# The same units on five engines, taken in another order: a kernel of four streams

## Chip, cores and metric

The kernel runs on one core of a Trainium2 chip. The time is the device time of one execution in microseconds; the kernel before took 561.78, 567.68 and 565.25 us in three runs, median 565.25.

## What is computed

128 sequences of 32 tokens with 128 features go through four layers; a conditioning vector of 128 features comes with each sequence. Cut to what matters:

```python
# layer 0: graph attention, twice (adjacency and its transpose), over the first 20 tokens
self_feat = concat(x, q if x.sum(-1) != 0 else 0) @ W_self.T + b_self
aff = where(adj.sum(-1) > 0, q_h @ k_h / sqrt(8), NEG) + adj @ w_bias + b_bias   # 16 heads
x = x + relu(self_feat + sum over d of (softmax(aff) @ self_feat[:20]) @ Wout[d])
# layer 1: x += gate * causal attention(modulated norm(x)); x += gate * (gelu(xm @ W1) @ W2)
# layer 2: x += gate * (gelu(xm @ w1) @ w2);  x += gate * (gelu_tanh(xm @ w1) @ w2)
# layer 3: as layer 1 without the causal mask
```

## The kernel before

The 128 sequences are eight chunks of 16, and a chunk is 512 token rows, held as tiles of 128 x 512 f32. Chunk c belongs to stream c % 4, so there are four streams, each with its own buffers and its own two banks of PSUM, and each does two chunks one after the other. A fifth lane holds the setup.

A chunk is a fixed list of stages (`chunk_stages`): the row sum and self product, keys and values, scores, softmax, turn (the transpose of the probabilities on DVE), values products, divide, and, for each of six blocks (attention, MLP with 4, 1 and 2 hidden products, attention, MLP with 4), stats, norm, modulate, then the attention's stages with gather and project, or the hidden products and down, and residual at the end. Each engine executes its own part of a stage; that part is a unit here. "Bias" is an addition on POOL (L678) of a gated bias that SP loads with the gate (`q_gate<-gates_out`, L570) before the block's residual (L682). `vals` on SP (L580) are four copies of the values into a block-diagonal tile, without which PE's values products can't start. `next_adj` (L529) loads the next chunk's 704 KB of adjacency.

What an engine does in which order is written out: `MERGE` has a string of digits for each engine, and each digit says from which lane (0 to 3 a stream, 4 the setup) the next unit is taken. Within a lane the order is that of the stages. `order` turns a string into a list of units, and at its end each engine's program is a loop over its list:

```python
def order(engine, merge):
    turns = [iter(lane) for lane in lanes(engine)]
    assert [merge.count(str(n)) for n in range(NS + 1)] == [len(lane) for lane in lanes(engine)]
    return [next(turns[int(s)]) for s in merge]
...
            for kind, a, c in ORDERS["gpsimd"]:
                stage(kind, a, c)
```

A unit begins with its waits for semaphores, which count what other engines and transfers have done for this stream, and a unit at the head of an engine's queue holds up all behind it. A PSUM bank is reused when its reader on ACT or DVE has counted: of four hidden products the fourth needs that the GELU (L798) of the second has run. ACT executes exponentials (L784), the GELUs of both kinds, tanh in the setup, and plain copies with scale and bias. The loops over these lists stand at L594 (SP), L692 (POOL), L801 (ACT), L974 (DVE) and L1183 (PE).

Of the kernel before, what the change touches and what calls it, by code (L numbers as in the profile page):

```python
# [160 lines left out]
def order(engine, merge):  # L161
# [2 lines left out]
    return [next(turns[int(s)]) for s in merge]  # L164

MERGE = {
    "tensor": ("001020420142012402044200420402042230011321302020103303221113013010120323112032000020123213212130"
               "310012112123220300103113210131203023032130112003222010313112330223120121100312302302213013033020"
               "110220223232303012320011233232310111021032122132312332310330223313131131213133023311322303201202"
               "122301132103232121312012330130311111323330331200101203013231121232331030101321331320312001012133"  # L170
               "0230312021120112301303032030223220200000"),
    "vector": ("000142201204041202400204200032030012012132203210320321021013120110310321122120323303210231110213"
               "310310100320233121330123021300213021200120100132321232123130123202312231003100212311333320323021"
               "310233020202212323110210202331312311130133133131232213232023201021113013313103102332031210313121"
               "2301320311322013330120131013310302130122312320230020102000320"),
    "scalar": ("444040044214240020404414224220404130120033210311033231012020000212312130101212320100332121011323"
               "002130102322101213303232111023200301123323001022322001330023232131112230212110333322131331132333"
               "101233212020231102133102223132103111132033331001203012311232103320131331103200321032120012131010"
               "323033220220000"),
    "gpsimd": ("120201020232104044203012010323123321102002010132103102020302131031001300122021201231231231220133"  # L180
               "212010021012013133031323023223230231003112321012312323301302312231310231233013212331013012321322"
               "31011231103232033110023113212123310123031213232013031303200021030101231033212020030320120"),
    "sync": ("020044402231101302230111202313000213232120010321022331123120331203331132202113031032131230130132"
               "21002031320"),
}
ORDERS = {engine: order(engine, merge) for engine, merge in MERGE.items()}

# [1057 lines left out]
```

## Time and profile before

| | |
|---|---|
| median of three runs | 565.25 us (561.78 to 567.68) |
| the profiled execution | 570.62 us, span 568.7 us |
| PE, DVE, ACT, POOL busy | 84%, 76%, 67%, 69% of the span |
| granted clock of TensorE, mean | 0.954 of full speed |
| DMA | 53.43 MB, q1 busy 31.5% of 16 engines |

A row of the timeline begins with the start and the duration in us, then engine, line, operation, tiles written and read, and count; what stands in brackets is the idle time of the engine before it and who ended it. PE is the matmuls, PEld their weight loads, DVE VectorE, ACT ScalarE, POOL GpSimd, SP SyncE, which only issues transfers.

### The profile page before, as it was taken

Reading aid. Unit: us, or ns where it says so; the run is one execution under the profiler, and the core shown is the slowest. Engines: PE = TensorE matmul, PEld = TensorE weight load, DVE = VectorE, ACT = ScalarE, POOL = GpSimd, SP = SyncE. Lnnn points to the kernel's source line nnn. Section 1 sums busy time; section 2 is a strip of 40 time slices with the busy share of each in tenths; the row PEclk is TensorE's granted clock in tenths of the full one; section 3 lists DMA queues with packets and bytes.
Section 4 is the critical chain, followed back from the end, with each engine's and each line's share of the span. In section 5 each row is a group of like instructions: output and inputs, shape, how many; then the busy total and the mean of one; then the engine's idle time right before and its main releaser. Section 6 shows DMA issues by size and latency. Waiting matters only on the chain.

```text
span 568.7 us, 21089 instructions
## 1 busy us (share of the span) xinstructions
PE 476.4 (84%) x9062; PEld 324.6 (57%) x9062; DVE 429.7 (76%) x914; ACT 383.0 (67%) x633; POOL 392.8 (69%) x408
## 2 busy tenths in 40 slices
PE   5877686898899789888899988767899988887996
PEld 2445354566557566465566555455576665565674
DVE  5888899899728856966899967898995454688841
ACT  7895375657587848666796836745866656686961
POOL 2768666667567879559887848655649899755546
PEclk9989898999599969999999987998999999899999
DMA  8514134123042620451433330212344232153321
GB/s 290 194 42 159 60 85 117 47 77 97 9 106 76 199 82 1 117 147 56 128 100 108 111 86 23 68 39 61 112 122 111 75 82 69 28 139 89 94 78 75
DMA packets 23468, 53.43 MB, mean 94 GB/s; under 512 B 5840, under 2 KB 8144, under 8 KB 23376
## 3 DMA queue, kind: packets, MB, share of 16 engines
q1 hardware_dynamic: 22912, 51.14, 31.5%
q8 instruction: 72, 1.18, 0.9%
q10 hardware_dynamic: 432, 0.94, 0.4%
q0 software_dynamic: 32, 0.01, 0.1%
q14 instruction: 20, 0.16, 0.1%
HBM read 39.74 MB, written 2.88 MB: 75 GB/s over the span
## 4 chain that ended last, share of the span: by engine, by line
POOL 27%; DVE 24%; PE 24%; issue 11%; ACT 6%; DMA 4%; SPq 4%; POOLq 0%; DVEq 0%; ACTq 0%
POOL x L682 5%; PE work L1169 5%; POOL x L678 4%; POOL rstd L672 4%; PE work L1178 4%; POOL xm L689 4%; DVE prob L932 4%; PE work L1128 4%; DVE mx L925 3%; POOL kbd L656 3%; POOL prob L667 2%; SPq L580 2%; PE work L1101 2%; DVE prob L927 2%; PE work L1048 2%
## 5 line engine op out<-in xcount | busy, mean ns | idle before, releaser
L793 ACT ACTIVATE xn<-x,nmr,rstd 128x128 f32<-128x128 f32 x192 | 78.5, 482 | 41.4 <-POOL nmr L675 41.3
L1169 PE MATMUL work<-xm,w_layer 128*128 128x512 f32 x176 | 91.5, 634 | 10.4 <-POOL xm L689 9.7
L1178 PEld LDWEIGHTS work<-w_layer,prob 128*128 128x128 f32 x704 | 83.0, 195 | 12.8 <-ACT prob L798 8.7
L1178 PE MATMUL work<-w_layer,prob 128*128 128x128 f32 x704 | 86.8, 280 | 2.3 <-ACT prob L798 2.2
L798 ACT ACTIVATE prob<-work,first 128x512 f32<-128x512 f32 x88 | 58.7, 684 | 42.7 <-PE work L1169 42.5
L678 POOL TENSOR_TENSOR x<-x,q_gate 128x512 f32<-128x512 f32 x48 | 60.8, 1273 | 31.7 <-DMA q_gate<-gates_out 31.7
L932 DVE STREAM_TRANSPOSE prob<-prob 128x1024 f32<-128x1024 f32 x64 | 78.4, 1232 | 2.5 <-ACT prob L784 2.5
L682 POOL TENSOR_TENSOR x<-x,q_gate 128x512 f32<-128x512 f32 x48 | 60.7, 1271 | 24.1 <-DVE q_gate L971 24.0
L689 POOL TENSOR_TENSOR xm<-turned_in,mod 128x512 f32<-128x512 f32 x48 | 50.6, 1056 | 30.1 <-DVE turned_in L966 30.1
L1128 PE MATMUL work<-vbd,prob 128*32 128x36 f32 x4096 | 52.6, 208 | 21.8 <-issue 10.2
L1128 PEld LDWEIGHTS work<-vbd,prob 128*32 128x32 f32 x4096 | 46.1, 117 | 41.1 <-issue 27.2
L784 ACT ACTIVATE prob<-prob 128x1024 f32<-128x1024 f32 (+1 forms) x64 | 56.2, 894 | 16.5 <-POOL prob L667 13.5
L956 DVE BATCH_NORM_STATS2 stats<-x 128x6 f32<-128x128 f32 x192 | 41.4, 278 | 27.2 <-POOL x L682 27.1
L971 DVE TENSOR_TENSOR q_gate<-work,q_gate 128x512 f32<-128x512 f32 x48 | 32.5, 681 | 35.3 <-PE work L1178 28.4
L667 POOL TENSOR_TENSOR prob<-prob,mx 128x640 f32<-128x640 f32 x32 | 40.7, 1271 | 24.3 <-DVE mx L922 24.2
L966 DVE TENSOR_TENSOR turned_in<-work,mod 128x512 f32<-128x512 f32 x48 | 32.5, 680 | 25.3 <-PE work L1144 25.3
L672 POOL TENSOR_TENSOR rstd<-veps,neg_half 128x4 f32<-128x4 f32 x48 | 48.8, 1017 | 3.7
L1169 PEld LDWEIGHTS work<-xm,w_layer 128*128 128x128 f32 x176 | 29.7, 196 | 37.0 <-POOL xm L689 15.3
L1144 PE MATMUL work<-ident,xn 128*128 128x128 f32 x192 | 41.3, 303 | 9.7 <-ACT xn L793 7.2
L1144 PEld LDWEIGHTS work<-ident,xn 128*128 128x128 f32 x192 | 25.4, 146 | 31.4 <-ACT xn L793 28.3
L925 DVE TENSOR_REDUCE mx<-work 128x32 f32<-128x1024 f32 x32 | 38.8, 1213 | 5.5 <-PE work L1101 5.5
L656 POOL TENSOR_TENSOR kbd<-turned_in,graph_mask 128x1280 f32<-128x1280 f32 x16 | 37.5, 2347 | 5.9 <-ACT turned_in L760 4.0
(138 smaller groups left out, 933.9 us busy)
## 6 DMA issues: line engine op xcount, KB each, us to landing
q_gate<-gates_out SPq DMA_DIRECT2D x192, 128.0 KB, 2.9
vbd<-v_ev SPq DMA_DIRECT2D x128, 72.0 KB, 2.4
kbd<-in_adj SPq DMA_DIRECT2D x8, 704.0 KB, 5.0
turned_in<-in_x_tok SPq DMA_DIRECT2D x8, 256.0 KB, 3.0
out_x<-x SPq DMA_DIRECT2D x8, 256.0 KB, 2.2
turned_in<-in_x_feat SPq DMA_DIRECT2D x7, 256.0 KB, 4.5
w_layer<-in_weights SPq DMA_DIRECT2D x2, 768.0 KB, 5.3
w_layer<-in_modw SPq DMA_DIRECT2D x1, 768.0 KB, 7.4
```

Of the source, the lines that this page charges most:

```text
L672: pool.tensor_tensor(rstd[s][:], veps[s][:], neg_half[:], ALU.pow).then_inc(pool_step[s], 1)
L678: pool.tensor_tensor(x[s][:], x[s][:], gate_bias[s], ALU.add).then_inc(biased[s], 1)
L682: pool.tensor_tensor(x[s][:], x[s][:], qT[s], ALU.add).then_inc(x_ready[s], 1)
L689: pool.tensor_tensor(turned_out, as_seqs(xm0[s][:]), shift.unsqueeze(3).broadcast_to([P, T, BT, S]), ALU.add).then_inc(xm_ready[s], 1)
L784: act.activation(e, e, ACT.Exp).then_inc(exped[s], 1)
L793: act.activation(xn[s][:, t], x[s][:, t], ACT.Identity, scale=rstd[s][:, t:t + 1], bias=nmr[s][:, t:t + 1]).then_inc(xn_ready[s], 1)
L798: act.activation(hT[s][u], bank(s, f"h{j}.{u}"), GELU[BLOCKS[j][3]], bias=vec(HID_BIAS[j], u)).then_inc(h_ready[s], 1)
L932: dve.transpose(e, e).then_inc(turned[s], 1)
L1128: last = pe.matmul(out_h[S * b:S * b + S, :, i * GH + h], block_of(s, att, (PG * pair + i) * GH + h, b), vbd[s][:, :, b * H + (PG * pair + ...
L1144: last = pe.transpose(bank(s, f"xn{a}")[:, t * P:(t + 1) * P], xn[s][:, t], ident[:])
L1169: pe.matmul(bank(s, f"h{j}.{u}"), w[UP[j]][:, 0, u * D:(u + 1) * D], xm[s][:], start=True, stop=True).then_inc(filled[s], 1)
L1178: last = pe.matmul(bank(s, f"y{a}")[:, t * D:(t + 1) * D], hT[s][u][:, t * P:(t + 1) * P], w[DOWN[a]][:, u], start=(u == 0 and t == 0), st ...
```

## The change

All five strings of `MERGE` are replaced. Each new string has the same number of each digit as the old one, so every engine executes the same units with the same instructions, waits and buffers, and within a stream in the same order; what differs is how the four streams and the setup are interleaved on each engine. Nothing else of the program is edited. The diff:

```diff
 MERGE = {
-    "tensor": ("001020420142012402044200420402042230011321302020103303221113013010120323112032000020123213212130"
-               "310012112123220300103113210131203023032130112003222010313112330223120121100312302302213013033020"
-               "110220223232303012320011233232310111021032122132312332310330223313131131213133023311322303201202"
-               "122301132103232121312012330130311111323330331200101203013231121232331030101321331320312001012133"
-               "0230312021120112301303032030223220200000"),
+    "tensor": ("001024010202240410220044201024402432001232120300103303212113013012301032231012000203031221212013"
+               "301022211221313021000313111301203320323010110203022210331112332321021121300312003202021303313012"
+               "010220223230323012320101323123023121210212310123323312331003223133131130132133123113232020331221"
+               "202131031233221201312102330130311111323330331212003013321121232303310101321331321320321001012313"
+               "0233012012102121031233003202032320200000"),
...
-    "scalar": ("444040044214240020404414224220404130120033210311033231012020000212312130101212320100332121011323"
-               "002130102322101213303232111023200301123323001022322001330023232131112230212110333322131331132333"
-               "101233212020231102133102223132103111132033331001203012311232103320131331103200321032120012131010"
-               "323033220220000"),
+    "scalar": ("444044004142024020401224422440404103122003310113033320112020000221331201102122310232100311011323"
+               "023010102322013112303321211322030010123330201022322010330032231231121222301131333022311331102333"
+               "311223230120123123310120321223103111132033331120030012311232033120131331012300321023120012113102"
+               "030332223020000"),
-    "gpsimd": ("120201020232104044203012010323123321102002010132103102020302131031001300122021201231231231220133"
-               "212010021012013133031323023223230231003112321012312323301302312231310231233013212331013012321322"
-               "31011231103232033110023113212123310123031213232013031303200021030101231033212020030320120"),
-    "sync": ("020044402231101302230111202313000213232120010321022331123120331203331132202113031032131230130132"
-             "21002031320"),
+    "gpsimd": ("120201020221300444203012021031332021312002011033102010220321030311031020202031210212123013121323"
+               "210200121012313103233130023223230213001321231012312230331323120233101230213331210231310213312323"
+               "22111031231032033212100131312123311032230131232013031320300020101013130322232321000021030"),
+    "sync": ("002044124230103123021021013320103201223111002030222330113201323123131323210132031320131203101323"
+             "21003202310"),
 }
```

The string of the vector engine, left out here, changes in the same way.

## Rows read from the trace of the kernel before

**Rows 1.** The page's busy times: us, share, instructions

```profile
PE 476.4 (84%) x9062; PEld 324.6 (57%) x9062; DVE 429.7 (76%) x914; ACT 383.0 (67%) x633; POOL 392.8 (69%) x408
```

**Rows 2.** Table of waits, POOL: us in total, times, longest

```profile
POOL x L678 <- DMA q_gate<-gates_out: 31.7, 13, 6.4
```

**Rows 3.** Chain that ended last: start, us, what

```profile
121.64 2.83 issue
...
243.23 5.89 DMA q_gate<-gates_out
...
333.40 2.15 issue
...
519.93 3.18 issue
```

**Rows 4.** Timeline of PE, places where its queue waits, and its tail

```profile
105.61 1.13 PE L1048 MATMUL work<-xm,w_layer 128*128 128x512 f32 x2 [1.43 <-POOL xm L689]
...
257.57 1.49 PE L1144 MATMUL work<-ident,xn 128*128 128x128 f32 x4 [1.90 <-ACT xn L793]
...
378.54 0.77 PE L1128 MATMUL work<-vbd,prob 128*32 128x36 f32 x64 [1.35 <-DVE prob L932]
...
526.72 1.98 PE L1169 MATMUL work<-xm,w_layer 128*128 128x512 f32 x4 [1.29 <-POOL xm L689]
...
544.51 1.16 PE L1155 MATMUL work<-w_layer,turned_in 128*128 128x128 f32 x8
...
556.63 3.79 PE L1169 MATMUL work<-xm,w_layer 128*128 128x512 f32 x8
560.42 3.81 PE L1178 MATMUL work<-w_layer,prob 128*128 128x128 f32 x32
```

**Rows 5.** Timeline of POOL, and one row of DVE

```profile
123.47 0.69 DVE L966 TENSOR_TENSOR turned_in<-work,mod 128x512 f32<-128x512 f32 x1 [0.55 <-PE work L1144]
...
124.50 1.28 POOL L678 TENSOR_TENSOR x<-x,q_gate 128x512 f32<-128x512 f32 x1 [2.87 <-DMA q_gate<-gates_out]
...
125.74 1.05 POOL L689 TENSOR_TENSOR xm<-turned_in,mod 128x512 f32<-128x512 f32 x1
...
249.19 3.73 POOL L678 TENSOR_TENSOR x<-x,q_gate 128x512 f32<-128x512 f32 x3 [5.17 <-DMA q_gate<-gates_out]
...
554.09 1.27 POOL L678 TENSOR_TENSOR x<-x,q_gate 128x512 f32<-128x512 f32 x1 [3.50 <-DMA q_gate<-gates_out]
```

**Rows 6.** Timeline of SP's issues

```profile
240.61 0.58 SPq L529 DMA_DIRECT2D kbd<-in_adj  x1
...
241.74 4.32 SPq L570 DMA_DIRECT2D q_gate<-gates_out  x8
...
331.60 2.42 SPq L580 DMA_DIRECT2D vbd<-v_ev  x4
```

**Rows 7.** The page's DMA issues: KB each, median us to landing

```profile
q_gate<-gates_out SPq DMA_DIRECT2D x192, 128.0 KB, 2.9
```

**Rows 8.** Groups by line, ACT's table loads: count, busy us, mean ns

```profile
L798 ACT ACT_TABLE_LOAD x22 | 28.2, 1283 | 0.4
...
L784 ACT ACT_TABLE_LOAD x15 | 19.2, 1283 | 0.3
L708 ACT ACT_TABLE_LOAD x1 | 1.3, 1283 | 2.1 <-issue 2.1
```

**Rows 9.** Timeline of ACT, around a table load and near 410 us

```profile
246.80 1.28 ACT L784 ACT_TABLE_LOAD   x1
248.09 2.00 ACT L784 ACTIVATE prob<-prob 128x1024 f32<-128x1024 f32 x2
...
408.40 0.60 ACT L776 ACTIVATE v_ev<-work 128x512 f32<-128x512 f32 x1
...
417.33 0.67 ACT L788 ACTIVATE turned_in<-work,zero_col 128x512 f32<-128x512 f32 x1
```

More of the change, by code:

```diff
@@ L172 @@
[L172 to L175, printed above, removed]
-    "scalar": ("444040044214240020404414224220404130120033210311033231012020000212312130101212320100332121011323"
-               "002130102322101213303232111023200301123323001022322001330023232131112230212110333322131331132333"
-               "101233212020231102133102223132103111132033331001203012311232103320131331103200321032120012131010"
-               "323033220220000"),
@@ L180 @@
-    "gpsimd": ("120201020232104044203012010323123321102002010132103102020302131031001300122021201231231231220133"
-               "212010021012013133031323023223230231003112321012312323301302312231310231233013212331013012321322"
-               "31011231103232033110023113212123310123031213232013031303200021030101231033212020030320120"),
-    "sync": ("020044402231101302230111202313000213232120010321022331123120331203331132202113031032131230130132"
-               "21002031320"),
+    "tensor": ("001024010202240410220044201024402432001232120300103303212113013012301032231012000203031221212013"
+               "301022211221313021000313111301203320323010110203022210331112332321021121300312003202021303313012"
+               "010220223230323012320101323123023121210212310123323312331003223133131130132133123113232020331221"
+               "202131031233221201312102330130311111323330331001212003013321121232303310101321331320321001012313"
+               "0233012012102121031233003202032320200000"),
@@ new lines @@
+    "vector": ("000411220204014022020402400033201002201322210130320132201301120301130121123221020333201231231013"
+               "103110120032303213312301200301201321020120103132023122132310120322312231010302012311330332230322"
+               "131033220021202323012002121331330121311131331231322123233023210211301013131303120323032110133121"
+               "2310323013120231332010131013310302130122132320223002000030120"),
+    "scalar": ("444044004142024020401224422440404103122003310113033320112020000221331201102122310232100311011323"
+               "023010102322013112303321211322030010123330201022322010330032231231121222301131333022311331102333"
+               "311223230120123123310120321223103111132033331120030012311232033120131331012300321023120012113102"
+               "030332223020000"),
```

## Prediction

> **What bounds the kernel now.** I read the busy table first: PE is busy 84% of the span, POOL 69%, ACT 67% [rows 1]. No engine is full, so what ends each stretch is a queue whose head waits while work behind it is ready. The table of waits says what ends those waits; the one that an order can mend most directly is POOL's for the gate loads, 31.7 us in 13 waits [rows 2]. Then I read the chain that ended last. It changes engine almost every microsecond, and the pieces called "issue" in it are time in which an engine stood at a wait. Four of them are heads of a queue: at 121.64, after the DMA of 243.23, at 333.40 and at 519.93 [rows 3]. Last I decoded the digits of the merges into units, for both kernels, and laid the old order beside the trace, so that every unit has its start and the time at which its last wait was satisfied. A unit is named here by its stage and chunk.
>
> At the end PE is the bound. From 526.72 it runs with hardly a gap until the last down product, and the last 3.8 us of matmul are followed by one multiply and one add; what is left of the span is the last store, and 1.9 us of the execution lie around the span [rows 4]. In that stretch a different order of PE's units gives nothing unless its inputs come late.
>
> **How much moves.** Each engine executes the same units, 424, 349, 303, 281 and 107 for PE, DVE, ACT, POOL and SP. Counted as pairs of units that change sides, 238, 173, 129, 166 and 72 pairs swap, and a unit moves by one place on average, at most 11. No stream gains or loses places for long: the change is local swaps all along, not another staggering.
>
> **Gains on the chain.** Four places, each costed by what PE or the next stage lost there.
> At 121.64 POOL's head is the bias add of chunk 2, which waits 2.87 us for its gate load; the shift add of chunk 1 stands behind it though its input is there from DVE's end at 123.47 + 0.69 = 124.16, and it starts at 125.74 [rows 5]. The bias goes three places later. Worth 1.6 us.
> At 244.02 POOL waits 5.17 us for the gate of chunk 0's last block. That load was issued at 241.74, behind chunk 2's 704 KB adjacency, and took 5.89 us where the median of 192 is 2.9 [rows 3, 5, 6, 7]. The bias goes five places later, past the residual and the statistics of chunk 3, which were what PE then waited for: 1.90 us before the transposes at 257.57 [rows 4]. Worth 1.90. On SP this gate is moved later too, past chunk 1's gate and its adjacency load, so it lands later; five places of POOL, some 6 us of 1.2 us operations, cover it. Uncovered it would cost the 5.17 again.
> At 333.40 PE's head is the values product of chunk 4, waiting 2.15 us for four copies that SP issued from 331.60 on, 35 us after the last thing they wait for, PE's products of the same chunk; SP's order now has it six places earlier and PE's has chunk 7's row sum in front [rows 3, 6]. Worth 2.15.
> At 519.93 POOL waits 3.18 us for chunk 6's gate and holds up chunk 5's shift add, for which PE idles 1.29 us [rows 3, 4]. The bias goes four places later. Worth 1.29.
> Sum 1.6 + 1.90 + 2.15 + 1.29 = 6.94. The bounds: zero, if the next wait in each place ends at the same time, and the waits themselves, 2.83 + 5.17 + 2.15 + 3.18 = 13.3. I take 6.94, since it is what the consumer behind the wait showed.
>
> **Gains off the chain.** Four more heads of PE's queue get a ready unit in front (chunk 2's queries at 104.19, chunk 1's gather at 146.96, chunk 5's turning at 361.42, chunk 7's values at 377.19): 1.43 + 1.45 + 1.45 + 1.35 = 5.68 us of idle PE [rows 4] (the first and the last of the four stand there). The chain runs through DVE there, so a filled gap helps only as far as PE is the next bound. Bounds 0 and 5.68; I take half, 2.84.
>
> **Cost: function tables of ACT.** The instructions of the program stay, but their order decides how often ACT changes its function table. The trace has 38 table loads, 22 in front of GELUs, 15 of exponentials, one at the start, of 1.283 us each [rows 8]. Reading ACT's order unit by unit with one table each for exp and tanh, for exact and for approximate GELU gives exactly these 22 and 15; the same reading of the new order gives 26 and 17. Six more, 7.7 us of ACT. They are four pairs more, near 215, 247, 308 and 410 us, less one pair in the tail. ACT was waiting for PE before the one near 215, and the two near 247 and 308 hold up only units that are late anyway: I charge 0.5 for the three. Near 410 ACT is dense: there the exponentials of chunks 4 and 5 now stand behind chunk 7's keys, and the gather evacuation of chunk 5 behind three loads. From 409.0, the end of chunk 7's values copy: three exponentials 3.0, load 1.28, GELU 0.69, load 1.28, two exponentials 2.0, load 1.28, GELU 0.69, so the gather copy starts at 420.2 instead of 417.33 [rows 9]. PE's fourth hidden product waits for that last GELU, which frees its bank, and chunk 5's projection behind it slips by 2.6. Charge 2.6. Bounds of all table loads: 0, and 7.7 with every one on the path.
>
> A load follows the activation before it within 0.02 us and the next activation starts at its end (246.80 + 1.28, next at 248.09) [rows 9]. The Trainium skill, ScalarE: Activation LUTs, section What ACT_TABLE_LOAD costs, has 1283 ns for the load and adds about 1380 ns of drain for every switch, and its rules for kernel authors say to group by table set, which speaks against this change. By the page six switches would be an estimated 16 us of ACT instead of 7.7. The trace agrees with the load and shows no drain beside it, so the sum goes by the row.
>
> **Cost: the tail.** POOL's last bias adds (chunk 7's, 6's, 5's of the last block, chunk 4's of the one before) now stand together in front of chunk 4's residual, which was issued at once before; four of 1.27 are 5.1 us [rows 5]. Chunk 6's last norm goes five places forward on PE. Laid out with the trace's durations from the last projection of chunk 6 on: its residual ends 1.7 us earlier, its statistics push chunk 7's scaling and chunk 4's second maximum back by 2.4, chunk 4's projection starts 2.2 later than 544.51, POOL is free of the biases at 547.5, and PE reaches chunk 4's last hidden products 1.3 us later than 556.63, having waited 0.8 for a transpose. The gate load of chunk 7 that POOL waited 3.50 for is now issued first, which saves nothing, since PE was busy then [rows 4, 5]. Charge 1.3, bounds 0 and 3.
>
> **Sum.** -6.94 - 2.84 + 0.5 + 2.6 + 1.3 = -5.4 us, on the profiled execution's 570.62: 565.2. That execution was 0.95% above the median of the three runs, so the forecast for a median is 565.25 x 565.2 / 570.62 = 559.9.
>
> **Rivals.**
> First, the whole chain wait is regained at each of the four places, and only half of the off-chain gaps: -13.3 - 2.84 + 4.4 = -11.8, or 553.6. For it: the same correction shows at many smaller places; SP's worst late issues are all moved forward, and 20 of 48 biases go later, 14 earlier. Against it: PE, 84% busy, was regularly the next to be late.
> Second, exchange: each mended wait is replaced by that of the unit now in front, 565. For it: of PE's 238 swapped pairs, 175 put forward a unit whose inputs came later in the old run than the other's. That number is tilted, because the old run's times were made by the old order, but it is a warning.
> Third, slower: ACT becomes the one that ends waits. The place is 405 to 422 us and every other place where two table loads surround one activation; the price is 6 x 1.283 = 7.7, with the tail's 1.3 it is +9.0, and the mended waits go into other waits: 579.6, or 574.2 as a median. It decides as soon as ACT has under 1.28 us of idle time in front of the added loads. For it, ACT's largest waits are for PE and POOL, so ACT is already in the loop of nearly all stages; against it, ACT is idle a third of the span [rows 1].
> That the change is not what it says, with "instructions as they were", is part of this third case: 38 loads become 44.
>
> **Chances.** The forecast case 0.46 (own range 556 to 564), full regain 0.17, exchange 0.16, slower 0.21. A measurement here can tell about 1%, below 559.6 or above 570.9. The forecast lies on the first line and gives 0.25 to faster and 0.21 to no change; full regain is all faster, exchange nearly all no change, the third nearly all slower: 0.42, 0.36, 0.22. The range has to hold most of the first three cases and half of the third: 547 (both upper bounds of the gains with only the 0.5 against them are 552.1 profiled, or 547) to 572.
>
> **What would show it.** In the changed kernel's page: 26 and 17 table loads, ACT busy up by about 7.7; POOL's wait for gate loads well under 31.7 us; no PE wait of 2 us near 333 before the values product, and no 5 us wait of POOL near 244; GELU and exponential alternating near 405 to 422 with a PE gap before the fourth hidden product; four bias adds in a row on POOL before chunk 4's last projection residual, and PE's last down product still at the end of an almost gapless stretch. The forecast is wrong if PE's idle time does not fall, if POOL's wait for gates is only moved, or if waits of PE for GELU outputs grow by more than a few us.

## The result and the profile after

The changed kernel took 577.12 us (median of four executions, 575.86 to 579.28) where the kernel before, beside it, took 566.46 (561.78 to 570.42). The ratio is 1.022, 95% interval 1.014 to 1.030: slower, where 559.9 was forecast; the interval leaves open whether by 2%. A later measurement on another chip (the control, below) gave 1.010, 1.003 to 1.018. Medians below are of all executions; the ratios, and the table of parts below, leave out those that lay more than 1.5% above the fastest of their kernel.

The profiled execution took 579.28 us, its span 577.5. The page's busy times, and from the table of waits two of POOL's, at lines 678 and 682:

```profile
PE 483.7 (84%) x9062; PEld 326.0 (56%) x9062; DVE 431.2 (75%) x914; ACT 391.8 (68%) x639; POOL 392.7 (68%) x408
```

```profile
POOL x L678 <- DMA q_gate<-gates_out: 32.1, 15, 7.3
...
POOL x L682 <- DVE q_gate L971: 29.3, 14, 7.5
```

Against [rows 1] ACT has six instructions and 8.8 us more, and PE 7.3 us more for the same 9062 matmuls. POOL's wait for gates has not moved: 32.1 us against 31.7 [rows 2], in two more pieces and with a longer longest one. PE's idle time, which had to fall, has not either: 577.5 - 483.7 = 93.8 us against 568.7 - 476.4 = 92.3. The groups by line give ACT's table loads, as read off the order before the run (26, 17 and one at the start):

```profile
L798 ACT ACT_TABLE_LOAD x26 | 33.4, 1283 | 0.5
...
L784 ACT ACT_TABLE_LOAD x17 | 21.8, 1283 | 0.3
L708 ACT ACT_TABLE_LOAD x1 | 1.3, 1283 | 2.1 <-issue 2.1
```

Near 244 us, where the forecast has POOL's bias add for chunk 0 moved out of its 5.17 us wait [rows 5], the timelines of POOL and of SP and the chain read:

```profile
246.41 1.27 POOL L678 TENSOR_TENSOR x<-x,q_gate 128x512 f32<-128x512 f32 x1 [0.70 <-DMA q_gate<-gates_out]
...
253.75 1.28 POOL L678 TENSOR_TENSOR x<-x,q_gate 128x512 f32<-128x512 f32 x1 [4.53 <-DMA q_gate<-gates_out]
255.17 2.51 POOL L682 TENSOR_TENSOR x<-x,q_gate 128x512 f32<-128x512 f32 x2
```

```profile
240.27 2.43 SPq L570 DMA_DIRECT2D q_gate<-gates_out  x4
242.74 0.42 SPq L529 DMA_DIRECT2D kbd<-in_adj  x1
243.21 0.43 SPq L526 DMA_DIRECT2D turned_in<-in_x_feat  x1
243.68 3.07 SPq L570 DMA_DIRECT2D q_gate<-gates_out  x4
246.79 0.42 SPq L529 DMA_DIRECT2D kbd<-in_adj  x1
```

```profile
246.33 7.35 DMA q_gate<-gates_out
```

The add is five places later, and POOL still stands 4.53 us for it. SP issues the load 1.9 us later than before [rows 6]. In the old order 704 KB of adjacency stood just ahead of it too (chunk 6's, at 240.61) and chunk 1's gate behind it; now chunk 1's gate and chunk 5's adjacency are ahead and chunk 6's adjacency is right behind. Its four issues take 3.07 us, and its last part 7.35 us instead of 5.89 [rows 3]. It lands at 253.7, the old one at 249.1. What the queue of POOL gave, the queue of SP took.

At 333.40, the second place of the old chain, the wait is gone: PE's timeline runs from the down product through chunk 7's row sum to chunk 4's values products (line 1128) without a gap.

```profile
334.54 3.74 PE L1178 MATMUL work<-w_layer,prob 128*128 128x128 f32 x32
338.12 1.02 PE L1028 MATMUL work<-turned_in,ones 128*128 128x512 f32 x2
339.07 0.77 PE L1091 MATMUL work<-kbd,q_gate 64*32 64x160 f32 x32
339.77 1.38 PE L1128 MATMUL work<-vbd,prob 128*32 128x36 f32 x128
```

Near 410 ACT does what the forecast says: three exponentials, load, GELU, load, two exponentials, load, GELU, and the gather copy late, at 426.72 instead of 417.33 [rows 9].

```profile
412.60 0.60 ACT L776 ACTIVATE v_ev<-work 128x512 f32<-128x512 f32 x1 [0.74 <-PE work L1056]
413.10 2.94 ACT L784 ACTIVATE prob<-prob 128x1024 f32<-128x1024 f32 x3
416.06 1.28 ACT L798 ACT_TABLE_LOAD   x1
417.35 0.69 ACT L798 ACTIVATE prob<-work,first 128x512 f32<-128x512 f32 x1
418.06 1.28 ACT L784 ACT_TABLE_LOAD   x1
419.35 2.01 ACT L784 ACTIVATE prob<-prob 128x1024 f32<-128x1024 f32 x2
421.38 1.28 ACT L798 ACT_TABLE_LOAD   x1
422.67 0.69 ACT L798 ACTIVATE prob<-work,first 128x512 f32<-128x512 f32 x1
426.72 0.69 ACT L788 ACTIVATE turned_in<-work,zero_col 128x512 f32<-128x512 f32 x1 [3.35 <-PE work L992]
```

But the gather copy did not wait for the loads: its gap of 3.35 us is ended by PE (line 992, the gather product). PE in turn stood in the middle of its last scores product, and from there on its matmuls take up to twice as long (1.92 us for the two of a hidden product that takes 1.02 elsewhere). The clock granted from 425 to 430 us is 0.50, that is 1.2 GHz of 2.4, after 1.00 from 410 to 420:

```profile
421.57 0.39 PE L1101 MATMUL work<-kbd,q_gate 32*32 32x128 f32 x10
423.71 1.92 PE L1101 MATMUL work<-kbd,q_gate 32*32 32x128 f32 x54 [1.75 <-issue]
425.56 1.11 PE L992 MATMUL work<-ident,xn 128*128 128x128 f32 x4
426.47 1.92 PE L1169 MATMUL work<-xm,w_layer 128*128 128x512 f32 x2
```

The tail is as before in kind: the last down product (3.81 us, as in [rows 4]) at the end of an almost gapless stretch, and four bias adds in a row, one and then three, ahead of chunk 4's last residual but one.

```profile
549.76 1.28 POOL L678 TENSOR_TENSOR x<-x,q_gate 128x512 f32<-128x512 f32 x1
551.89 3.73 POOL L678 TENSOR_TENSOR x<-x,q_gate 128x512 f32<-128x512 f32 x3 [0.86 <-DMA q_gate<-gates_out]
555.77 1.26 POOL L682 TENSOR_TENSOR x<-x,q_gate 128x512 f32<-128x512 f32 x1
```

**Where the time went.** I cut each trace at three events that every order has: the end of chunk 0's last residual on POOL (about 257 us), the end of chunk 7's fourth scores product on PE (about 370), and the end of the last of the first residuals of chunks 4, 5 and 7 (about 433); the fourth part ends with the last residual of all. The times are ends of rows of the timelines, and the kernels of the experiments below give several samples of each. With the same order in it a part still varies by 2 to 6 us between executions, so one trace alone says little.

| part | before | after | old order, all such executions | new order, all such |
|---|---|---|---|---|
| 1: to 257 | 258.2 | 256.5 | 256.6 (11; 254.4 to 258.9) | 256.9 (5; 255.1 to 259.6) |
| 2: to 370 | 113.1 | 118.8 | 110.3 (10; 108.6 to 113.1) | 116.3 (6; 114.5 to 118.8) |
| 3: to 433 | 61.1 | 69.2 | 63.2 (9; 61.1 to 64.9) | 68.4 (3; 67.6 to 69.2) |
| 4: to the end | 133.9 | 130.6 | 133.3 (12; 130.8 to 136.7) | 131.2 (6; 129.5 to 132.8) |

New less old, on the means: +0.3, +6.0, +5.3, -2.1, together +9.5 us. Parts 2 and 3 are the loss; in both the ranges of old and new do not touch. Half of it is idle time of PE, on the means 16.2 us instead of 13.0 in part 2 and 12.0 instead of 9.0 in part 3. The other half is PE being busy for longer, 2.8 and 2.3 us, at a lower granted clock. Part 1, with two of the forecast's four chain gains, is worth nothing.

### The profile page after: what moved, and what is told of

It reads as the page before. It is cut to its first block, busy times and chain, and to the rows that moved or that the text cites. A ratio compares the mean times of both kernels' runs of the same rounds, so it can differ in the third digit from the quotient of the medians.

```text
span 577.5 us, 21095 instructions
## 1 busy us (share of the span) xinstructions
PE 483.7 (84%) x9062; PEld 326.0 (56%) x9062; DVE 431.2 (75%) x914; ACT 391.8 (68%) x639; POOL 392.7 (68%) x408
## 4 chain that ended last, share of the span: by engine, by line
POOL 26%; PE 26%; DVE 22%; issue 12%; ACT 5%; DMA 4%; SPq 3%; POOLq 0%; DVEq 0%
POOL x L682 5%; PE work L1169 5%; POOL x L678 5%; DVE prob L932 5%; POOL xm L689 4%; POOL rstd L672 4%; PE work L1128 4%; PE work L1101 3%; SPq L570 3%; DMA q_gate<-gates_out 2%; PE work L1048 2%; DVE prob L919 2%; PE work L1178 2%; PE work L1091 2%; DVE stats L956 2%
## 5 line engine op out<-in xcount | busy, mean ns | idle before, releaser
L1169 PE MATMUL work<-xm,w_layer 128*128 128x512 f32 x176 | 95.4, 657 | 11.6 <-POOL xm L689 9.9
L678 POOL TENSOR_TENSOR x<-x,q_gate 128x512 f32<-128x512 f32 x48 | 60.8, 1274 | 32.1 <-DMA q_gate<-gates_out 32.1
L784 ACT ACTIVATE prob<-prob 128x640 f32<-128x640 f32 (+1 forms) x64 | 56.4, 897 | 22.0 <-POOL prob L667 10.9
L1169 PEld LDWEIGHTS work<-xm,w_layer 128*128 128x128 f32 x176 | 30.0, 198 | 39.5 <-POOL xm L689 16.2
L1101 PE MATMUL work<-kbd,q_gate 32*32 32x128 f32 x2048 | 38.2, 275 | 7.4 <-issue 4.5
L1144 PE MATMUL work<-ident,xn 128*128 128x128 f32 x192 | 39.5, 299 | 5.1 <-ACT xn L793 3.1
L1091 PE MATMUL work<-kbd,q_gate 64*32 64x160 f32 x1024 | 27.3, 319 | 17.5 <-issue 7.0
```

The costliest lines, as they stand in the source:

```text
L678: pool.tensor_tensor(x[s][:], x[s][:], gate_bias[s], ALU.add).then_inc(biased[s], 1)
L784: act.activation(e, e, ACT.Exp).then_inc(exped[s], 1)
L1101: last = pe.matmul(heads[:, :, b * n:(b + 1) * n], qT[s][rows_g, q // BT, q % BT * S:q % BT * S + S], by_head(s, a)[rows_g, :, q * n:(q + ...
L1169: pe.matmul(bank(s, f"h{j}.{u}"), w[UP[j]][:, 0, u * D:(u + 1) * D], xm[s][:], start=True, stop=True).then_inc(filled[s], 1)
```

## Experiments

The orders can be spliced: take one order's units that begin before a time in its trace, then the remaining ones in the other order. Each hybrid does so on all five engines unless it is said otherwise; the diffs show SP's string where that is short enough to follow, and the other engines' strings change by the same rule. The sum of the hybrids need not be the whole, since each has seams.

**1. The new order up to 250 us only.**

```diff
-    "sync": ("020044402231101302230111202313000213232120010321022331123120331203331132202113031032131230130132"
+    "sync": ("002044124230103123021021013320103201223111002032022331123120331203331132202113031032131230130132"
```

> All five engines take the new order for the units that begin before 250 us, the old order for the rest. Theory P (the loss of the new order is made in two places, a small one at 270 to 320 us and the large one at 376 to 431 us, by exponentials, a copy issue and GELUs that stand behind later ones; the gains before 250 us are real): about 5 us faster than the kernel before, ratio 0.99, since the trace of the changed kernel leads by 2 to 8 us in all chunks at 250. Rival L (the lead is given back wherever the stream of work next meets its full engine, so no local gain survives): ratio 1.00. Rival T (each table load costs its 1.28 us; this order has 42, four more than the old): 5 us slower, ratio 1.01.

569.24 us beside 568.01, ratio 1.003 (1.000 to 1.006). The 5 us did not come. In its trace POOL's late bias add again waits for the gate, 2.93 us, and chunk 0's last residual starts at 256.53, 0.4 us earlier than before, though chunk 3's residual ahead of it was 5.9 us early. Rival L's number came. A mechanism for it could be that chunk 0 is followed by chunk 4 in its stream, so that the other chunks' lead is worth nothing while chunk 0's gate is late; experiments 13 and 18 test that.

**2. The new order from 250 to 375 us only.**

```diff
-    "sync": ("020044402231101302230111202313000213232120010321022331123120331203331132202113031032131230130132"
+    "sync": ("020044402231101302230111202313000213232120011030222330113201323123131332202113031032131230130132"
```

> New order only for the units that the changed kernel begins between 250 and 375 us, old order before and after. Theory P: 3 to 5 us slower than before (the traces' lag of chunk 3 and 1 grows by 8 to 10 us between 270 and 320, part of it taken back by 375), ratio 1.005 to 1.01. Rival L: 1.00. Rival T (40 table loads, two more): 2.6 us slower, 1.005.

575.66 beside 568.01, ratio 1.016 (1.012 to 1.021): a loss larger than any theory gave (theory P had it at 1.005 to 1.010). Two more table loads are 2.6 us, a third of the measured 7.65.

**3. The new order from 375 to 431 us only.**

```diff
-    "sync": ("020044402231101302230111202313000213232120010321022331123120331203331132202113031032131230130132"
+    "sync": ("020044402231101302230111202313000213232120010321022331123120331203331132210132031032131230130132"
```

> New order only for the units that begin between 375 and 431 us. Theory P: most of the loss, 8 to 10 us slower than before, ratio 1.014 to 1.018. Rival L (the loss was a chance meeting of many small shifts and does not belong to a stretch): 1.00. Rival T (40 table loads, two more): 2.6 us slower, 1.005.

574.53 beside 568.01, ratio 1.013 (1.008 to 1.018). That is near what theory P gives, with five units of SP in another order, 21 digits of PE's string, and 15, 18 and 11 of the strings of DVE, ACT and POOL. But it is not most of the loss: the stretch before it costs as much (experiment 2).

**4. The changed kernel with the old order from 375 to 431 us.** The reverse of experiment 3: SP's `...131323210132031...` becomes `...131332202113031...`.

> The changed kernel with the old order put back between 375 and 431 us alone. Theory P: 8 to 10 us faster than the changed kernel's 577, so 567 to 569, ratio to the kernel before 1.00 to 1.005. Rival L: 1.02 as the changed kernel. Rival T (43 table loads, one less than the changed one): 1.3 us less than the changed kernel, 1.018.

572.01 beside 568.01, ratio 1.012 (1.006 to 1.018). By the medians that is some 5 us less than the changed kernel's 577.12, not 8 to 10; beside the control's ratio of 1.010 it is no gain at all. In its trace part 3 is back to 62.0 us, and part 2 stays long, 116.5 us.

**5 and 6. No table switches, in either order.** Both kernels with Tanh in place of the two GELUs; the GELU is left out.

```diff
-        GELU = {"Gelu": ACT.Gelu, "Gelu_apprx_tanh": ACT.Gelu_apprx_tanh}
+        GELU = {"Gelu": ACT.Tanh, "Gelu_apprx_tanh": ACT.Tanh}
```

> The kernel before with Tanh in place of both GELUs, so that ACT has no reason to change its function table between them and the exponentials; everything else as it was. Left out: the GELU itself, so the output is another. The price of 37 table loads in the old order. Theory P (ACT idles a third of the span, the loads mostly fill gaps): 567 to 562 us, ratio 0.99 to 1.00, provided that a Tanh takes as long as a GELU; any theory that puts the loads on the path: 37 x 1.28 = 47 us of ACT less and some 20 us or more off the time, ratio under 0.965.

> The changed kernel with Tanh in place of both GELUs. To be compared with the old order's Tanh kernel of this call. Theory T (the six more table loads make the loss of 10 us): the two differ by 2 us or less, ratio of the two under 1.005. Theory P (head of queue waits by the order itself, in the two stretches after 250 us): they still differ by 7 us or more, ratio 1.012 or more.

The old order with Tanh took 569.46 beside 568.04, ratio 1.001 (0.998 to 1.005); the new order with Tanh 577.60, ratio 1.014 (1.009 to 1.020). The page and the groups by line of the first:

```profile
PE 476.9 (84%) x9062; PEld 323.3 (57%) x9062; DVE 429.3 (76%) x914; ACT 335.2 (59%) x596; POOL 392.7 (69%) x408
...
L708 ACT ACT_TABLE_LOAD x1 | 1.3, 1283 | 2.1 <-issue 2.1
```

All 37 loads between the two functions are gone, ACT is busy 47.8 us less than in [rows 1], and the kernel is no faster. The GELU's replacement costs the same per row (58.9 us for 88 against 58.7). And the two orders differ by 1.4% without any switch, as much as with them. The interval leaves at most 0.2%, 1.3 us, as the price of all 37 on this kernel's path, so the six more cannot be the loss. This is the clearest result of the study.

**7 and 8. Which engine's order costs in 375 to 431 us.** Experiment 3's hybrid with ACT's string as before; and the kernel before with the new order there on ACT and PE alone.

```diff
-               "101233220120123123310120321223103111132033331001203012311232103320131331103200321032120012131010"
+               "101233212020231102133102223132103111132033331001203012311232103320131331103200321032120012131010"
```

> The stretch of 375 to 431 us in the new order on PE, DVE, POOL and SP, with ACT's old order; the hybrid with all five engines new there measured 1.013 (+7.4 us by fast runs). Theory A (ACT's order is what costs: exponentials of chunks 4 and 5 behind chunk 7's keys, more table loads): 1.00 to 1.004. Rival S (the order of SP and PE costs, chunk 4's values copies behind chunk 5's and its scores product behind chunk 6's work): still 1.010 or more.

> The stretch of 375 to 431 us in the new order on ACT and PE alone, with DVE, POOL and SP in the old. Theory A: 1.010 or more. Rival S: 1.00 to 1.006, as SP's and POOL's part is missing.

Without ACT's part 577.39 us, ratio 1.012 (1.006 to 1.018), so theory A falls: with ACT's old order the stretch is as slow or slower (part 3 is 74.9 us in its trace). With ACT and PE alone 588.59, ratio 1.037 (1.032 to 1.043), part 3 87.1 us. Rival S missed it, and theory A's "1.010 or more" holds in words, but nothing in it gives such a size. The orders of one stretch belong together: a string that fits its four fellows can cost 20 us with the wrong ones.

**9, 10 and 11. SP alone, PE alone, and all but SP, in the same stretch.** The three edits are the SP line of experiment 3, PE's line below, and experiment 3 without its SP line.

```diff
-               "...223313131131213133023311322303201202"
-               "122301132103232121312012330130311111..."
+               "...223313131131213133023311322020331221"
+               "202131031233221201312102330130311111..."
```

> The kernel before with SP's new order alone in the stretch of 375 to 431 us: five units, chunk 5's values copies before chunk 4's, chunk 6's gate last of the five. Theory SP (chunk 4's copies stand behind chunk 5's, which are ready 12 us later, and all that follows in chunk 4 is late): most of the stretch's loss, ratio 1.008 or more. Rival PE (the order of the products costs): 1.00 to 1.004.

> The kernel before with PE's new order alone in the stretch of 375 to 431 us. Rival PE: 1.010 or more (with ACT's new order beside it it measured 1.037, so the two or one of them costs more when DVE, POOL and SP stay). Theory SP: under 1.005.

> The stretch of 375 to 431 us in the new order on PE, DVE, ACT and POOL, SP in its old order. Theory SP: 1.00 to 1.004, the copies of chunk 4 are issued as before. Rival PE: 1.010 or more.

SP alone: 571.47 beside 569.46, 1.002 (0.998 to 1.007). PE alone: 582.99, 1.025 (1.019 to 1.031). All but SP: 572.48, 0.999 (0.993 to 1.006), a ratio that rests on five of twelve executions; by medians of all it is 1.005, where experiment 3 has 1.011. So the four compute engines' new orders, together, cost at most 0.6% in this stretch by either number, and with SP's more, as theory SP has it. But SP's alone does not cost the 0.8% that the same theory gives it, and PE's alone costs 2.5% where it allows 0.5%. In the hybrid with SP alone SP's timeline and PE's read:

```profile
401.69 5.76 SPq L580 DMA_DIRECT2D vbd<-v_ev  x8
```

```profile
409.02 1.19 PE L1128 MATMUL work<-vbd,prob 128*32 128x36 f32 x64 [1.51 <-issue]
```

Chunk 4's four copies are issued with chunk 5's, at 404.2, where the kernel before issues them at 387.73, and PE's values product of chunk 4 waits 1.51 us for them. Two other issues are late by the same knot, chunk 6's gate by 16.6 us and, on POOL, chunk 4's gate, for which POOL stands 8.89 us (6.39 before).

That is the old order of PE, though. In the new one chunk 4's values product stands later in PE's queue, and it does not wait for the copies: with SP's late order (experiment 3) and with SP's old one (experiment 11) it stands 0.30 us for DVE. The two traces part elsewhere, in how long the same matmuls take. Experiment 3, then 11:

```profile
412.40 0.77 PE L1128 MATMUL work<-vbd,prob 128*32 128x36 f32 x64 [0.30 <-DVE prob L932]
...
419.63 1.92 PE L1169 MATMUL work<-xm,w_layer 128*128 128x512 f32 x2
```

```profile
406.83 0.77 PE L1128 MATMUL work<-vbd,prob 128*32 128x36 f32 x64 [0.30 <-DVE prob L932]
...
411.74 1.02 PE L1169 MATMUL work<-xm,w_layer 128*128 128x512 f32 x2
```

PE idles 11.2 us of part 3 in the first and 11.6 in the second; part 3 is 68.5 and 63.4 us, and the granted clock 0.88 and 0.97. The second profiled execution was the fastest of its twelve, 562.73 us. So that SP's order adds to the loss is measured; that it does so by the wait for the copies is not what these traces show.

**12. The new order from 431 us on.**

```diff
-    "sync": ("...203331132202113031032131230130132"
-               "21002031320"),
+    "sync": ("...203331132202113031320131203101323"
+             "21003202310"),
```

> Old order up to 431 us, new order from there to the end on all engines: 37 table loads less one, the four bias adds in front of chunk 4's last projection residual, chunk 6's gate late bias at 520. The forecast's own terms here: 1.29 us gained near 520 and 1.3 us lost in the tail, ratio 1.00. From the traces (the changed kernel's lag falls from +10 to +8.7 us over this stretch): 0.997. Rival (every stretch of the new order costs, because it is laid out for other arrival times): 1.005 or more.

570.95 beside 569.46, ratio 1.005 (1.001 to 1.009). Nothing is gained from the last third, and it costs 0.1 to 0.9%, as the rival has it. By the means of the traces the part is 2 us shorter, but there the ranges of old and new overlap (130.8 to 136.7 and 129.5 to 132.8); I take the measurement.

**13. Chunk 0's gate first, in experiment 1's hybrid.** SP's 41st to 44th units: from chunk 1's gate, chunk 5's adjacency, chunk 4's input, chunk 0's gate to chunk 4's input, chunk 0's gate, chunk 1's gate, chunk 5's adjacency. (The expectation calls chunk 4's input chunk 0's; stream 0 loads it for its next chunk.)

```diff
-    "sync": ("002044124230103123021021013320103201223111002032022331123120331203331132202113031032131230130132"
+    "sync": ("002044124230103123021021013320103201223100112032022331123120331203331132202113031032131230130132"
```

> The hybrid with the new order up to 250 us (1.003 of the kernel before) with one edit on SP: chunk 0's input load and the gate load of its last block go two places forward, ahead of chunk 1's gate and chunk 5's 704 KB of adjacency. Theory G (POOL's late bias add still waits 2.9 us there because the gate lands 5.9 us later than before, which eats the lead): the wait goes and 3 to 4 us come back, ratio 0.995 to 0.998. Rival L (a lead before 250 us is given back later whatever ends it): still 1.003.

567.70 beside 570.61, ratio 0.998 (0.994 to 1.002); experiment 1 had 1.003. That is theory G's number, but the intervals of the two overlap, and they were on different chips. POOL's timeline shows what happened:

```profile
251.65 1.27 POOL L678 TENSOR_TENSOR x<-x,q_gate 128x512 f32<-128x512 f32 x1 [4.21 <-DMA q_gate<-gates_out]
...
254.41 1.27 POOL L678 TENSOR_TENSOR x<-x,q_gate 128x512 f32<-128x512 f32 x1
```

Chunk 0's add at 254.41 no longer waits. Chunk 1's, which stands ahead of it, now waits 4.21 us instead. The wait went to the neighbour whose load I had put second, and part 1 is as long as in experiment 1, 257.1 us against 257.8.

**14. The changed kernel with one edit on SP near 400 us.** Chunk 4's copies and chunk 6's second gate ahead of chunk 5's copies, as in the old order.

```diff
-    "sync": ("002044124230103123021021013320103201223111002030222330113201323123131323210132031320131203101323"
+    "sync": ("002044124230103123021021013320103201223111002030222330113201323123131323202113031320131203101323"
```

> The changed kernel with one edit on SP: chunk 4's values copies of the third attention and chunk 6's second gate go ahead of chunk 5's copies, as in the old order (the changed kernel measured 1.022). Theory SP (these two issues, 17 us later than their inputs allow, make the stretch of 375 to 431 us cost): 6 to 8 us less, ratio 1.008 to 1.012. Rival (the products' and exponentials' order would hold chunk 4 back anyway): 1.020 or more.

571.56 beside 570.61, ratio 1.002 (0.999 to 1.006), better than theory SP's 1.008. In the changed kernel POOL stood 7.32 us for chunk 6's gate at 420.84; here that add starts at once, at 407.74, but the unit behind it, chunk 5's residual, now waits 12.23 us for DVE instead of 7.55. It looked as if two units out of 1464 had been the whole loss. But part 3 of its trace is 66.5 us against 68.4 with the new SP order: only 2 us are explained. Hence the control below.

**15 and 16. Inside 250 to 375 us.** The new order for the units from 293 to 325 us alone, and from 250 to 375 without those.

```diff
-    "sync": ("020044402231101302230111202313000213232120010321022331123120331203..."
+    "sync": ("020044402231101302230111202313000213232120010321022330113201233123..."
```

> New order only for the units that begin between 293 and 325 us. Theory PE (in this almost gapless stretch of PE the new order puts chunk 4's third scores and chunk 1's third hidden product, which nothing waits for, ahead of chunk 6's second scores and chunk 3's projection, which are then 5.5 us late): 4 to 6 us slower than before, ratio 1.008 to 1.010. Rival (the 1.6% of 250 to 375 us is made outside, where self product and adjacency of chunk 7 and 5 are moved): 1.000 to 1.003.

> New order from 250 to 375 us but for the units between 293 and 325 us, which are taken in the old order; the whole stretch in the new order measured 1.016. Theory PE: 1.004 to 1.008. Rival: 1.014 or more.

568.15 beside 570.61, ratio 0.999 (0.995 to 1.003); and 572.40, ratio 1.003 (0.999 to 1.006). Theory PE falls for the first: the product moved behind others at 305 us costs nothing by itself (part 2 is 109.3 us). Its rival falls for the second: without these units the rest costs nothing sure either (111.8). Together the two sets cost 1.6% (115.8; experiment 2, on another chip). Which pairs across the seam make it, these runs don't tell.

**17. Control: the changed kernel again.** No edit.

> The changed kernel itself again, beside the kernel before on one chip. If the edit on SP removed the loss: 1.018 to 1.024 as at first (576 to 580 us). If the loss was mostly of the first chip and its few executions: 1.005 to 1.012, and then the edit on SP is worth far less than 2%.

575.36 beside 567.50, ratio 1.010 (1.003 to 1.018), by medians of all executions 1.014. The loss is confirmed; its size is 1.0 to 2.2% and nearer the lower end than the first four executions had it. Experiment 14's edit is then worth some 0.8% (1.002 against 1.010), not 2%, and since these two intervals overlap and the chips differ, perhaps nothing.

**18. The changed kernel with three edits.** Both edits on SP, and on POOL chunk 1's bias add behind chunk 2's residual, which is what experiment 13's trace asked for.

```diff
-               "210200121012313103233130023223230213001321231012312230331323120233101230213331210231310213312323"
+               "210200121012313103233300213223230213001321231012312230331323120233101230213331210231310213312323"
...
-    "sync": ("002044124230103123021021013320103201223111002030222330113201323123131323210132031320131203101323"
+    "sync": ("002044124230103123021021013320103201223100112030222330113201323123131323202113031320131203101323"
```

> The changed kernel with three edits: on SP chunk 4's copies and chunk 6's second gate ahead of chunk 5's copies (with this alone 1.002); on SP chunk 0's last gate ahead of chunk 1's gate and chunk 5's adjacency; on POOL chunk 1's bias add behind chunk 2's residual, because in the hybrid with the gate moved POOL then waited 4.2 us for chunk 1's gate instead. Theory G (three mended waits free the 3 to 4 us of lead near 250): 0.993 to 0.998. Rival L (a lead is taken back by the next stretch in which PE is full): 1.000 to 1.003.

570.11 beside 567.50, ratio 1.006 (1.002 to 1.011). The three waits are mended. POOL's gate waits fell by 13 us; in the same table its waits for DVE's gated product at line 682 rose from 24.0 us before the change to 34.3:

```profile
POOL x L682 <- DVE q_gate L971: 34.3, 15, 13.4
...
POOL x L678 <- DMA q_gate<-gates_out: 18.7, 12, 4.2
```

Its timeline

```profile
248.04 1.27 POOL L678 TENSOR_TENSOR x<-x,q_gate 128x512 f32<-128x512 f32 x1
249.46 1.28 POOL L682 TENSOR_TENSOR x<-x,q_gate 128x512 f32<-128x512 f32 x1
251.48 1.27 POOL L682 TENSOR_TENSOR x<-x,q_gate 128x512 f32<-128x512 f32 x1 [0.75 <-DVE q_gate L971]
252.71 1.27 POOL L678 TENSOR_TENSOR x<-x,q_gate 128x512 f32<-128x512 f32 x1
```

has chunk 0's last residual end at 250.7, 7.5 us before the old one. Still it is slower than the kernel before, by 0.2 to 1.1%: part 2 is 117 us, the new order's usual length, so that by 370 the lead is spent (367.8, where the old order's means add up to 366.9). Theory G's number is refuted, though its three waits are gone. Rival L's number is missed as well, and this is no test of its reason: against the new order's own mean for the end of part 2, 373.2, the lead is still there at 367.8. And experiment 14, without the two edits on the gates, had 1.002; the gates' edits added nothing that these runs can tell.

No version here is shown to beat the kernel before. The best, experiments 13 and 15, are at 0.998 and 0.999 with 1 inside the interval.

## Why the prediction was wrong

**The gain at 244.02, and the sentence that it is "covered" (1.90).** This is the first step that failed. The working had both queues in it: POOL's add five places later, SP's load also later, "five places of POOL, some 6 us, cover it. Uncovered it would cost the 5.17 again". It was not covered: 4.53 us. The five places were needed twice. POOL came to the add at 249.22 instead of 244.02, 5.2 us later; the load landed 4.6 us later, at 253.7 instead of 249.1; so of the old wait of 5.17 only 0.6 was gained. The 5.2 us could cover the old wait or the load's delay, not both, and the working put no number on the delay. Experiments 13 and 18 bear this out: with the load ahead of chunk 1's gate and of both adjacencies it lands in 6 us or less from its first issue, and the add doesn't wait.

**The other gains.** At 121.64 the wait moved: the same kind of add stands 3.27 us at 119.07. At 333.40 the wait really is gone, and part 2 is longer all the same. At 519.93 the late add runs at once, and part 4 may be 2 us shorter in the traces, but experiment 12 finds no gain. Summed over the four, POOL's total for gates went from 31.7 to 32.1, which the prediction had named as a sign against it. The sum of 9.8 us of gains was a sum of waits removed, each with its consumer's idle time; experiment 18, where 13 us of the gate waits are gone, 10 us of other waits have come, and the time is no better than experiment 14's, speaks against adding them up.

**The exchanges (0 in the sum, the second rival at 565).** This is the second and the larger failure. Parts 2 and 3 cost 11 us on the means, and the sum had nothing there but table loads. The working had the warning, 175 of PE's 238 swapped pairs put forward the unit with the later input, and priced it at a wash. In 375 to 431 us SP's order is part of the cost (experiments 3, 11 and 14, less surely than the rest): chunk 5's copies go ahead of chunk 4's, which are issued at 405.43 instead of 387.73, and chunk 6's gate goes behind both, at 416.38 instead of 398.78. The prediction had only that SP's worst late issues are all moved forward. Which unit hands the delay on is not shown: the copies have landed at 409.9, and PE takes them at 419.52; POOL's 7.32 us for the gate are followed by 7.55 for chunk 5's residual. "The change is local swaps all along" was true and said nothing on the price: five units of SP in another order beside matching swaps elsewhere make 1.3%.

**The table loads (3.1, and 7.7 as the bound).** The counts were exact and the price wrong. It is at most 1.3 us for all 37, from experiment 5, and the two orders differ as much without any (experiment 6). One sum in it is wrong too: 409.0 and the seven terms after it make 419.2 and not 420.2, which is what the trace has as their length (413.20 to 423.36), so the slip charged with 2.6 us was 1.9 by its own terms. The third rival, 574.2 us, has nearly the measured time, by luck: ACT's waits near 410 are for PE, and replacing its order made the stretch no faster (experiment 7). That ACT "is in the loop of nearly all stages" was no evidence that its load time is.

**The tail (1.3).** As a sequence it is right, four adds in a row; its 1.3 us lie within the 0.1 to 0.9% that experiment 12 has for all from 431 us on.

**The clock, not in the sum at all.** The windows of 380 to 430 us, before and then after; behind the POOL column stands the granted clock, then the DMA share and GB/s:

```profile
380.00:430.00 50.00, 43.91 (x1222) 31.30 (x1221) 44.34 (x76) 32.54 (x50) 27.03 (x31) 0.97 0.29 85
```

```profile
380.00:430.00 50.00, 38.26 (x1030) 25.87 (x1028) 38.60 (x65) 30.55 (x45) 19.57 (x23) 0.83 0.30 81
```

PE idled more there and its granted clock fell from 0.97 to 0.83. In the two profiles as wholes, 7.3 of the 8.8 us that the span grew by are PE being busy for longer with the same 9062 matmuls. Over whole executions the changed kernel had 0.937 to 0.948, mean 0.942, and 0.947 in the control; the kernel before had a mean of 0.954 in 17 beside experiments 5 to 8. Within those 17 a lower clock by 0.01 goes with 2.9 us more, with a correlation of only -0.57; at that slope 0.012 would be some 3 of the 10 us. The clock by itself is not the loss: experiment 1 had a mean of 0.947 too, PE busy 482.6 us in its trace, and lost 0.3%. That the idle time pulled the clock down was not tested alone, so this share is argued, not shown.

**What stays open.** Which swaps in 250 to 375 us make part 2 longer by 6 us: they need units on both sides of 293 or 325 us. By what wait SP's order costs in 375 to 431 us. And what experiment 14's edit is worth: its trace shows 2 us. So where the loss is made is shown, and that it is not the table loads; the swaps that make it are not.

## What to carry to other kernels

A wait at the head of a queue is shared property of the queue that waits and the queue that feeds it: before booking a gain for moving the waiter, lay out the feeder's new order with its bytes, and take the old wait and the new delay of the transfer together; the same places can cover only one of them. When the orders of several engines are replaced together, treat the sum of mended waits as an upper bound and not as an estimate; look as well for the units that go backward relative to their inputs, the DMA queue's among them. And before charging an engine's extra work, check that it ends somebody's wait: 48 us less of ACT was worth nothing here.

## What the runs showed of the hardware

A switch of ACT's function table took 1.283 us on the mean of the 37 and of the 43, in the rows shown with 0.02 us or less beside it, and all 37 together cost the kernel nothing measurable. A gate load of 4 x 128 KB took 10.0 us from its first issue to its landing with 704 KB of adjacency issued 1 us ahead of it and as much again right behind its last part (the changed kernel, 243.68 to 253.68). It took 7.4 us with 704 KB ahead and another gate behind (the kernel before, 241.74 to 249.13), and 5.6 us ahead of both adjacencies (experiment 18, 240.34 to 245.91). At a granted clock of 0.50 two matmuls of 128x512 took 1.92 us, and 1.02 at the full clock. The kernel before, executed again and again on one chip, varied by 1.8% (562.56 to 572.84 us in 17 executions), which sets how small a difference can be told at all.
